# Masked row maxima of four query tiles: one add-and-maximum instruction on VectorE in place of mask matmuls

## The reference

```python
def causal_attn(q, k, v, scale):
    T = q.shape[1]
    mask = jnp.tril(jnp.ones((T, T), dtype=bool))
    s = jnp.einsum('bthd,bshd->bhts', q, k) * scale
    s = jnp.where(mask[None, None], s, jnp.finfo(s.dtype).min)
    p = jax.nn.softmax(s, axis=-1)
    return jnp.einsum('bhts,bshd->bthd', p, v)
...
attn1 = causal_attn(q1, k1, vcat, scale)
attn2 = causal_attn(q2, k2, vcat, scale)
attn = attn1 - lambda_full * attn2
...
x = x + s * g      # s: attention branch, g: gate from the expert branch
```

## Time and profile before

| | |
|---|---|
| median of 3 runs | 2013.88 us (2012.34 to 2017.2) |
| profiled execution, outside | 2012.9 us |
| profiled execution, span | 2010.8 us |
| TensorE (PE) busy | 1871.5 us, 93% |
| VectorE (DVE) busy | 1465.0 us, 73% |
| ScalarE (ACT) busy | 1050.6 us, 52% |
| max matmuls (L903) | 1536 |
| mask matmuls (L907) | 1024 |
| maxima (L1786) | 1536 |

### The profile page before, as it was taken

How to read it: one execution, slowest core, us unless ns; L and a number is a source line. 1 busy time by engine, 2 the same in 40 slices (tenths; PEclk the granted TensorE clock), 3 DMA queues, 4 the chain that set the end, 5 groups by cost and what they waited for, 6 DMA issues and landing times. The chain is left out here.

```text
span 2010.8 us, 42110 instructions
## 1 busy us (share of the span) xinstructions
PE 1871.5 (93%) x11851; PEld 1117.8 (56%) x11851; DVE 1465.0 (73%) x3476; ACT 1050.6 (52%) x2538; POOL 676.0 (34%) x728
## 2 busy tenths in 40 slices
PE   6888999999999999999999999999899999999975
PEld 4543434444443443444434347777788888778864
DVE  7888888888888888888888854444368855433358
ACT  2325667677676666766666644443333322344444
POOL 4542441111112232232322214776603432233334
PEclk9977999999999999999999999999999999999997
DMA  4443342211223121121212103443312112244362
GB/s 124 140 144 101 99 131 55 69 51 44 69 54 86 42 62 49 50 61 40 64 42 59 40 12 97 125 124 121 117 42 100 69 53 67 90 129 129 98 235 106
DMA packets 196456, 170.43 MB, mean 85 GB/s; under 512 B 92120, under 2 KB 176392, under 8 KB 195976
## 3 DMA queue, kind: packets, MB, share of 16 engines
q1 hardware_dynamic: 177304, 119.95, 21.1%
q0 software_dynamic: 15888, 46.16, 6.5%
q10 hardware_dynamic: 3168, 3.15, 0.5%
HBM read 104.16 MB, written 72.70 MB: 88 GB/s over the span
## 5 line engine op out<-in xcount | busy, mean ns | idle before, releaser
L1786 DVE TENSOR_REDUCE mx<-ps 128x1 f32<-128x512 f32 (+3 forms) x1536 | 762.3, 549 | 104.1 <-PE ps L907 81.1
L1376 ACT ACTIVATE fbuf<-ps 128x512 f32<-128x512 f32 (+3 forms) x1024 | 459.2, 508 | 247.8 <-PE ps L918 234.2
L903 PE MATMUL ps<-rbuf 72*128 72x512 bf16 (+3 forms) x1536 | 503.5, 335 | 31.0 <-DVE mx L1786 20.2
L918 PE MATMUL ps<-rbuf 75*128 75x512 bf16 (+3 forms) x1536 | 499.3, 332 | 19.0 <-DMA rbuf<-mrows 17.2
L918 PEld LDWEIGHTS ps<-rbuf 75*128 75x128 bf16 x1536 | 149.9, 98 | 324.3 <-ACT fbuf L1376 143.4
L1376 ACT ACTIVATE gbuf<-ps 128x512 f32<-128x512 f32 (+2 forms) x512 | 210.2, 470 | 105.4 <-PE ps L918 85.9
L752 POOL TENSOR_SCALAR_AFFINE_SELECT gbuf<-gbuf 128x512 f32<-128x512 f32 x96 | 61.5, 641 | 530.1 <-ACT gbuf L1376 530.1
L903 PEld LDWEIGHTS ps<-rbuf 72*128 72x128 bf16 x1536 | 151.4, 99 | 146.8 <-DVE mx L1786 101.8
L933 PE MATMUL ps<-fbuf 128*32 128x512 f32 (+3 forms) x2048 | 229.1, 520 | 3.6 <-ACT fbuf L1365 0.8
L907 PE MATMUL ps<-maskq,identb 128*128 128x128 bf16 x1024 | 229.3, 224 | 0.0
L759 POOL DMA_INDIRECT y_scr<-wstage,bidx x138 | 139.1, 1008 | 245.3 <-ACT wstage L1420 221.5
(11 more groups left out here) (274 smaller groups left out, 2981.7 us busy)
## 6 DMA issues: line engine op xcount, KB each, us to landing
rbuf<-q_scr SPq DMA_DIRECT2D x192, 96.0 KB
xs_scr<-in_pad SPq DMA_DIRECT2D x8, 1360.0 KB, 6.2
gbuf<-xs_scr SPq DMA_DIRECT2D x69, 136.0 KB
gbuf<-xe_scr SPq DMA_DIRECT2D x69, 136.0 KB
rbuf<-k_scr SPq DMA_DIRECT2D x192, 48.0 KB
gbuf<-y_scr SPq DMA_DIRECT2D x8, 1024.0 KB
q_scr<-gbuf SPq DMA_DIRECT2D x48, 128.0 KB
gbuf<-a_scr SPq DMA_DIRECT2D x12, 512.0 KB, 4.8
```

What stands on the lines that cost most here:

```text
L903: ins = pe.matmul(o, qst[par][0:PROWS, i // 4, m, P * (i % 4):P * (i % 4 + 1)], kst[par][0:PROWS, m % 2, 512 * piece:512 * piece + width], ...
L918: pe.matmul(o, kst[par][0:SROWS, m % 2, P * j:P * (j + 1)], qst[par][0:SROWS, h, m, t0:C], start=True, stop=True).then_inc(b_scores, 1)
L1376: act.activation(prob(s)[:, t0:C], ps[:, s % SRING, t0:C], ACT.Exp, scale=SCALE).then_inc(b_exp, 1)
L1786: dve.tensor_reduce(mx[:, i // 4, piece, n:n + 1], ps[:, SRING + s % SRING, 0:width], AX, ALU.max, negate=True).then_inc(b_maxed, 1)
```

## The change

The maxima of the masked pieces of tiles 4 to 7 no longer have their mask added by TensorE. One VectorE instruction, `tensor_tensor_reduce` with ALU operations add and max, adds a table `allowed` (128x512 fp32: 0, and -1e30 above the diagonal in its last 128 columns, of which the last `width` columns are read), writes the sum back into the PSUM bank, and takes the row maximum into `mx[:, 1, 1]`, not negated. The masked pieces of tiles 0 to 3 keep their mask matmul.

In `MAXJ`, piece and map change places: for each map, piece 0 and then piece 1. VectorE's maximum of a piece 0 waits for two max matmuls, its own and that of the piece 1 behind it, and the instruction for the piece 1 has no wait of its own. `shift_full` multiplies by -1 and takes the minimum in one instruction. GpSimd fills `allowed` (one memset, one affine select), and `consts_ready` counts to 7.

```diff
 MAXJ = [(i, 0, m) for i in range(4) for m in range(MAPS)] + \
-       [(i, p, m) for i in range(4, 8) for p in range(2) for m in range(MAPS)]
+       [(i, p, m) for i in range(4, 8) for m in range(MAPS) for p in range(2)]
...
+        allowed = sb("allowed", [P, C])
...
-            sp.wait_ge(consts_ready, 6)
+            sp.wait_ge(consts_ready, 7)
...
+                st.done(pool.memset(allowed[:, :], 0.0))
...
+                pool.affine_select(out=allowed[:, C - P:], in_=allowed[:, C - P:], pattern=[[-1, P]],
+                                   compare_op=ALU.is_ge, fill=NEG, base=0, channel_multiplier=1).then_inc(consts_ready, 1)
...
-            pe.wait_ge(consts_ready, 6)
+            pe.wait_ge(consts_ready, 7)
...
-                diag = piece == i // 4
+                diag = i < 4
...
             def reduce_max(u, s):
                 i, piece, m = MAXJ[s]
                 width = min(512, P * (i + 1) - 512 * piece)
-                dve.wait_ge(b_maxs, JOBS * u + s + 1)
                 n = 4 * m + i % 4
+                if piece == 1:
+                    scores = ps[:, SRING + s % SRING, 0:width]
+                    dve.tensor_tensor_reduce(scores, scores, allowed[:, C - width:C], 1.0, NEG, ALU.add, ALU.max,
+                                             mx[:, 1, 1, n:n + 1]).then_inc(b_maxed, 1)
+                    return
+                both = 1 if i >= 4 else 0
+                dve.wait_ge(b_maxs, JOBS * u + s + 1 + both)
                 dve.tensor_reduce(mx[:, i // 4, piece, n:n + 1], ps[:, SRING + s % SRING, 0:width], AX, ALU.max,
                                   negate=True).then_inc(b_maxed, 1)
...
-                dve.tensor_tensor(mx[:, 1, 0], mx[:, 1, 0], mx[:, 1, 1], ALU.min).then_inc(b_mfull, 1)
+                dve.scalar_tensor_tensor(mx[:, 1, 0], mx[:, 1, 1], -1.0, mx[:, 1, 0], ALU.mult, ALU.min).then_inc(b_mfull, 1)
...
+            dve.wait_ge(consts_ready, 7)
             for s in range(LEAD):
                 reduce_max(0, s)
```

## The result

The changed kernel takes 2102.99 us (median of 4 runs, 2098.06 to 2105.98) against 2013.11 us (the kernel before, median of 4 runs): the ratio on record, which is not the quotient of the two medians, is 1.043, 95% interval 1.0405 to 1.0456. The profiled execution's span is 2103.0 us, 92.2 us over the 2010.8 us of before.

A forecast was written before the change was run, and what follows sets the result against it. The prediction took the TensorE–VectorE loop handing three banks to and fro as the bound: 68 us for the units, 2 for the start and 14 for the instruction make 84, giving 2098 us on the median 2013.9; range 2065 to 2146.

The forecast's parts named there:

- The loop through the value matmuls: VectorE's even maximum waits through value matmuls, next scores and partner matmul; TensorE then waits for banks: 2.2 us a unit, 68 us.
- the nine groups that change: Groups of four steps, 0 to 7 and 20 to 47, whose lengths the prediction followed; steps 8 to 19 were called unchanged.
- d: Extra cost of one add-and-maximum over a plain reduction on VectorE: taken as 0.066 us, at most about 0.19.
- the old price: The sequence worked out with the new instruction costing no more than the plain reduction, d = 0.
- The term of 14 us: Odd maximum's end stands in the loop about seven times a unit, so d adds 7 x 31 x 0.066.
- rival "separate accumulator": Accumulator read is a separate VectorE instruction as on ScalarE, d = 0.187: 2125 us, chance 0.15.
- half-rate rival: Add-and-maximum streams at half rate; seven places add about 2.9 us a unit, 91 in all: 2175 us, chance 0.07.
- Steps 36 to 39: Group with 256-column partners: second max matmul waits for maximum 29 behind the shift rows' 1.56 us; worked out 3.55 us.
- the 43 jobs ahead: Max jobs ahead of the first unit, without scores or value matmuls: 1.4 us more, say 2 with the first unit.
- the sequence with d: Hand-followed unit, 2.2 us longer with d = 0, plus 0.066 us at about seven places of the loop.
- The cover of the constants: Extra GpSimd fill and selection at 34 us have 25 us of cover; without it about 1 us once.
- The rival on the other side: TensorE sets the pace and the pair hides; 512 mask matmuls come off at 0.055 us: 1986 us, chance 0.08.

The follow-up runs named there:

- the kernel with d = 0: Changed kernel, masked pieces of tiles 4 to 7 reduced by a plain maximum without their mask, order and double wait kept: 2093.9 us, ratio 1.0375.
- The run of the pair alone: Kernel before with only the new job order and the double wait; mask matmuls and plain reductions stay: 2103.1 us, ratio 1.0415.
- the run with own waits for ten pairs: Changed kernel, double wait removed from the eight pairs cut by the value matmuls and from jobs 24/25 and 28/29: 2010.38 us, ratio 0.9977.
- own waits everywhere: Changed kernel in its new order, but every maximum waits for its own matmul only: 2005.49 us, ratio 0.994.
- the run of the instruction alone: Kernel before with its old order and single waits, add-and-maximum replacing the mask matmuls of tiles 4 to 7: 2018.48 us, ratio 1.0.
- the first of the two with the mask left out: Kernel before with new order, single waits, plain reductions, mask left out of the maxima of tiles 4 to 7: 1982.93 us, ratio 0.9845.
- last run: Kernel before with new order, single waits, plain reductions, mask left out of the maxima of tiles 0 to 3 too: 1976.04 us, ratio 0.9784.

## Why the prediction was right

- **The loop through the value matmuls.** Worked out from rows 4 to 7, it gives each of the nine groups that change to 0.16 us or better, and in the kernel with d = 0 eight of the nine to 0.03. The sum of the nine is 25.8 us with the old price, 26.2 with d, measured 26.1. The run of the pair alone shows the cause, the run with own waits for ten pairs shows the places.
- **The price of the instruction.** I took d = 0.066 us between -0.02 and 0.19. The accumulator is indeed read by a row of its own, as on ScalarE. The Trainium skill's page "VectorE: DVE Perf Modes" states in "Two Vector instructions with no wait between them" that an instruction which also writes out its accumulator is two instructions; the changed kernel's trace agrees, with 512 such reads of 140 ns. But the read of 140 ns starts before the main row ends: 256 columns start at 543.28 or 544.22 and the reads at 543.62 and 544.56, so a maximum ends 0.48 us behind its start against 0.41, d = 0.07. That d came out at the value taken is luck: 0.066 was the price of another instruction's extra operand, and the main row here is no dearer than a two-input one; the 0.07 is the end of the read. The term of 14 us had seven places in it; the run with the plain reduction shows six, 13 us (steps 36 to 39 lose 0.07 us, not twice that). I expected 15 of that run, and the medians give 9. The rival "separate accumulator", 2125 us, had the right fact and the wrong size, because it priced the read at ScalarE's 187 ns and laid it end to end. (The half-rate rival's own places, three of 256 columns and two each of 384 and 512, sum to 2.7 us a unit and 83 us, not 2.9 and 91. Nothing hangs on it: the main rows run at the plain rate.)
- **Steps 36 to 39.** The one group that is off by more than 0.1 us (3.55 against 3.39, and against 3.32 with d = 0): the shift rows' four instructions took 1.56 us in the rows I used (538.95 to 540.51) and 1.39 in the changed kernel (545.29 to 546.68 in its timeline). That is 0.17 of the 0.23 us; the rest stays open.
- **The first units.** Here the step failed: I took 2 us for the 43 jobs ahead and unit 0 together. The 43 jobs took 26.4 us against 24.2 (2.3 more), unit 0 55.5 against 45.6, unit 1 38.8 against 33.1. That is 18 us against 2 + 2.2 worked out for these. In unit 0 most of it goes with the double wait: the unit takes 54.7 us in the run of the pair alone and 47.1 with own waits everywhere. VectorE also does the routing of the experts there, which is a likely reason, not a tested one. But the granted clock, for which the prediction has no term, is in it as well: 0.77 in unit 0 before, 0.69 with own waits, 0.62 in the changed kernel. And unit 1's 5.7 us are mainly the clock. Its first 15 us run at the lower level:

```profile
210.00:225.00 15.00, 15.00 (x77) 6.14 (x70) 8.86 (x26) 7.09 (x16) 6.34 (x9) 0.50 0.38 106
```

  In the run of the pair alone unit 1 runs at full clock and takes 34.8 us, hardly more than its later units (34.4); in the run of the instruction alone, which has no double wait, it takes 38.5 us at a mean clock of 0.82.
- **The units 2 to 30.** They took 66.4 us more, 2.3 a unit, where the sequence with d gives 2.7. The medians above give 2.6. The rest is what the kernel before lost itself and the changed one doesn't: single units of it took 35.6 and 34.4 us against a usual 31.4, because the first max matmul of a unit waited 1.8 and 2.1 us for its k load and the granted clock was lower for some us behind that. This surplus in the prediction (2.7 against 2.3 in 29 units, about 10 us) cancels most of the lack in the first units (14 us). Outside the units there are 2.2 us more ahead of the attention and 5.3 more behind its last scores matmul (809.2 us to the end before, 814.5 after), in stages that the change doesn't touch; no run says why. That 2098 comes so close to 2103 is in part luck.
- **The cover of the constants** held: the last new fill and selection end at about 36 us, and the first load that waits for them is issued at 60.31 us against 60.30 before. The attention's first matmul starts at 128.7 us against 126.5, but that start moves without the constants too (127.5 in the run of the pair alone, 130.9 in the first of the two with the mask left out).
- **The rival on the other side** (TensorE sets the pace, 1986 us) needed the loop to be 0.3 us shorter. Its term was right in size: with single waits, the new order and nothing in the masks' place the kernel is at 1982.93 us. With the add-and-maximum and waits of their own ahead of it, it is at 2005.49. So of the 28 us that the removed matmuls are worth, the instruction and its late start behind a wait take back more than half even where no pair waits.

## What to carry to other kernels

Two engines that hand a small ring of buffers to and fro lose little by an instruction that is a little dearer (0.07 us where the ring waits for it), but they can lose much of a stretch of other work if a consumer waits for two items and the producer does that work between them. Before waits are merged, write down what the producer runs between the two items, and what the consumer has queued behind the first; where neither was long, the merged wait was free (six pairs of sixteen here); elsewhere it cost between nothing and 0.6 us a group of four steps here, less than the 1.00 us of the value matmuls. The removed work, 16 short matmuls of 0.055 us a unit, has to be read by starts and not by its 224 ns of duration. And read the granted clock of each stretch before a stretch's length is put down to a wait: unit 1 here was longer by 5.7 us, mainly by the clock.

## What the runs showed of the hardware

- An add-and-maximum over a PSUM operand and an SBUF table, written back to PSUM, takes 290, 418, 556 and 690 ns at 128, 256, 384 and 512 columns, plus a 140 ns accumulator read that overlaps the main row's end; together 0.07 us longer than a plain reduction.
- With 32 of these in a unit instead of 16, each with a semaphore instruction ahead, VectorE stood idle for 2.9 us at a turn of its loop, the instruction queue's packets went from 49 to 120, and for 7 to 10 us after such a turn TensorE's granted clock was 0.5 (1.2 GHz). In the 12 us ahead of the fall TensorE had been busy for 8.98 us; in the 57 us at full clock for 53.34.
- The granted clock also fell to 0.50 behind waits of TensorE for a load: behind 3.43 us for 25 us (last run, 280 to 305), behind 1.77 us from 268 to 272 us (the kernel before).
- A wait on a semaphore instruction ahead of the add-and-maximum let it start 0.19 us behind the matmul's end, where a reduction's own wait took 0.04; whether by the semaphore instruction or by the add-and-maximum's own start isn't separated.
